# Four graph layers: tiles on 512-byte lines, and the third layer's wide product in blocks of 384, 384 and 260 columns

## The reference

```
h = maximum(layernorm(x), 0); x = x + L0(h, adj)   # attention, 8 heads, 6 static masks, 2 from adj
h = maximum(layernorm(x), 0); x = x + L1(h, adj)   # attention, 4 heads, masked by adj
h = maximum(layernorm(x), 0); x = x + L2(h, adj)   # graph attention, 4 heads:
    Wh = h @ W.T + bW;  e = Wh @ attn;  A = tanh(where(adj, e @ Wh.T, 0));  hp = relu(A @ Wh)
    ha = concat(hp) @ A_w.T;  hf = h @ fc_w.T
    coeff = sigmoid(hf @ g1_w.T + ha @ g2_w.T + gbias);  L2 = hf * coeff + ha * (1 - coeff)
h = maximum(layernorm(x), 0); x = x + L3(h, adj)   # attention times a cosine adjacency, 8 heads
```

## The kernel before, in words

| tile | start mod 512 | used as |
|---|---|---|
| ln_hT_hi, ln_hT_lo | 416 | moving and weights, all layers |
| square_w_hi, _lo | 416 | moving and weights, second and fourth layer |
| l0_w_hi, _lo | 480 | moving and weights, first layer |
| l0_oT, l1_oT | 256 | weights, output projections |
| l2_g_w_hi, _lo | 480 | weights |
| l2_wh_w_hi, l2_wh_w_lo | 480, 0 | moving; rows of 4112 bytes, so a second row lies 16 bytes further |
| l2_cat, l2_ha, l2_hf (hi, lo) | 416 | moving |
| l2_aw, l2_sq (hi, lo) | 32 | weights |
| same_batch | 192 | weights |

## Time and profile before

### The profile page before, as it was taken

One profiled execution on the slowest core, in us unless ns is written; L12 is line 12 of the kernel. 1 busy time (PEld: TensorE's weight loads), 2 busy tenths in 40 slices (PEclk: granted clock), 3 DMA queues, 4 the chain that ended last, 5 costly groups with the idle time before them and its releaser, 6 DMA issues. The chain is left out here.

```text
span 2171.3 us, 52286 instructions
## 1 busy us (share of the span) xinstructions
PE 2089.0 (96%) x18300; PEld 1881.0 (87%) x18300; DVE 1494.9 (69%) x3312; ACT 1002.0 (46%) x2057; POOL 504.2 (23%) x562
## 2 busy tenths in 40 slices
PE   7999999799999889999999999999999899999997
PEld 6888888699999789999999999999998778777786
DVE  6877878677777545555555555555554799999997
ACT  5666666454555322222222222222222476667665
POOL 3222222222222011111111110111111444444442
PEclk9999999999999899999999999999999999999999
DMA  3222222333222201111001001111110121122111
GB/s 90 80 71 63 74 68 65 118 113 84 81 82 86 68 21 31 31 30 30 30 30 30 25 20 30 30 30 30 30 30 20 42 61 51 53 59 59 55 49 45
DMA packets 149370, 113.31 MB, mean 52 GB/s; under 512 B 42944, under 2 KB 148800, under 8 KB 149312
## 3 DMA queue, kind: packets, MB, share of 16 engines
q1 hardware_dynamic: 149312, 112.52, 18.1%
HBM read 78.93 MB, written 33.55 MB: 52 GB/s over the span
## 5 line engine op out<-in xcount | busy, mean ns | idle before, releaser
L273 POOL TENSOR_TENSOR ln_rstd<-ln_var_eps,minus_half 128x2 f32<-128x2 f32 x128 | 90.9, 710 | 1106.2 <-DVE ln_var_eps L266 1106.2
L1615 ACT ACTIVATE l_cat_hi<-banks 128x512 fp32r<-128x512 f32 x128 | 76.5, 597 | 260.4 <-PE banks L1788 260.4
L161 PE MATMUL banks<-ln_hT_hi,square_w_hi 128*128 128x256 f32 x512 | 154.8, 302 | 5.0 <-DVE square_w_lo L614 3.2
L290 ACT ACTIVATE ln_h<-ln_x,ln_shift,ln_rstd 128x256 f32<-128x256 f32 x256 | 139.4, 592 | 32.0 <-DVE ln_shift L280 23.3
L161 PE MATMUL banks<-ln_hT_hi,l_g_w_hi 128*128 128x256 f32 x512 | 149.3, 292 | 4.9 <-POOL l_a_bd L1568 4.9
L163 PE MATMUL banks<-ln_hT_hi,square_w_lo 128*128 128x256 f32 x512 | 146.0, 285 | 0.0
L162 PE MATMUL banks<-ln_hT_lo,square_w_hi 128*128 128x256 f32 x512 | 145.7, 285 | 0.0
L161 PE MATMUL banks<-l_cat_hi,l_aw_hi 128*128 128x256 f32 x512 | 144.2, 282 | 1.4 <-DVE l_cat_lo L1675 1.4
L163 PE MATMUL banks<-l_cat_hi,l_aw_lo 128*128 128x256 f32 x512 | 144.1, 281 | 0.0
L162 PE MATMUL banks<-l_cat_lo,l_aw_hi 128*128 128x256 f32 x512 | 143.8, 281 | 0.0
L163 PE MATMUL banks<-ln_hT_hi,l_g_w_lo 128*128 128x256 f32 x512 | 143.1, 279 | 0.0
(11 more groups left out here) (227 smaller groups left out, 6910.8 us busy)
## 6 DMA issues: line engine op xcount, KB each, us to landing
hidden<-y SPq DMA_DIRECT2D x96, 256.0 KB, 2.2
ln_x<-hidden SPq DMA_DIRECT2D x96, 256.0 KB, 2.8
x_res<-hidden SPq DMA_DIRECT2D x96, 256.0 KB, 2.9
ln_x<-x SPq DMA_DIRECT2D x32, 256.0 KB, 2.9
x_res<-x SPq DMA_DIRECT2D x32, 256.0 KB, 3.0
out<-y SPq DMA_DIRECT2D x32, 256.0 KB, 2.2
l_adj_u<-adj SPq DMA_DIRECT2D x96, 16.0 KB, 2.4
l_stage_attnT<-L_attnT SPq DMA_DIRECT2D x4, 256.0 KB, 3.3
```

What stands on the lines that cost most here:

```text
L161: nc.tensor.matmul(out, lhs(lh), rhs(rh), start=start, stop=False, skip_group_check=True)
L273: self.nc.gpsimd.tensor_tensor(self.rstd[:, g.slot], self.var_eps[:, g.slot], self.core.minus_half[:, 0:PAIRS], ALU.pow).then_inc(self.rst ...
L290: last = self.nc.scalar.activation(self.h[:, u, p, :], self.x[:, u, p, :], ACT.Relu, bias=self.shift[:, u, p:p + 1], scale=self.rstd[:, u, ...
L1615: nc.scalar.activation(cat_hi[:, h * KC:(h + 1) * KC], halves(B_HP[h]), ACT.Relu).then_inc(cat_hi_ready.sem, 1)
```

## The change

Every SBUF tile is now asked for through `tile`, which places those with at least 128 elements a partition at a multiple of 512 bytes and smaller ones at 32. The rows of the third layer's wide weights (hi and lo) are lengthened from 1028 to 1152 columns and the rows of wh from 1028 to 1152, so that the second row begins on a multiple of 512 bytes as well; the added columns are neither written nor read. The wide product is cut at 384 and 768. The bias row keeps its 1028 columns. The same two-argument replacement stands at every place that makes a tile; the diff below leaves repeats out.

```diff
+LINE = 512
+
+
+def tile(nc, name, shape, dtype):
+
+    return nc.sbuf_tensor(name, shape, dtype, align_bytes=LINE if math.prod(shape[1:]) >= P else 32)
...
-        self.x_res = ctx.enter_context(nc.sbuf_tensor("x_res", [P, 2, PAIRS, D], F32))
-        self.y = ctx.enter_context(nc.sbuf_tensor("y", [P, 2, PAIRS, D], F32))
+        self.x_res = ctx.enter_context(tile(nc, "x_res", [P, 2, PAIRS, D], F32))
+        self.y = ctx.enter_context(tile(nc, "y", [P, 2, PAIRS, D], F32))
...
-        sb = lambda n, shape, dt=F32: ctx.enter_context(nc.sbuf_tensor(f"ln_{n}", shape, dt))
+        sb = lambda n, shape, dt=F32: ctx.enter_context(tile(nc, f"ln_{n}", shape, dt))
...
-        H, CH, WC = 4, 4 * KC, 4 * D + 4
+        H, CH, WC = 4, 4 * KC, 4 * D + P
...
-        self.wh_bias = sb("wh_bias", [P, WC])
+        self.wh_bias = sb("wh_bias", [P, 4 * D + 4])
...
-    THIRDS = ((0, 344), (344, 344), (688, WC - 688))
+    THIRDS = ((0, 384), (384, 384), (768, WC - 768))
...
-        wh = sb("wh", [P, PAIRS, WC])
+        wh = sb("wh", [P, PAIRS, H * D + P])
```

More of the change, by code:

```diff
@@ L1 @@
+import math
 from contextlib import ExitStack
@@ L320, in __init__ @@
     def __init__(self, core, ctx, tag, raw):
-        sb = lambda n, shape, dt=F32: ctx.enter_context(core.nc.sbuf_tensor(f"{tag}_{n}", shape, dt))
+        sb = lambda n, shape, dt=F32: ctx.enter_context(tile(core.nc, f"{tag}_{n}", shape, dt))
         self.raw = sb("w_raw", [P, raw, KC, D])
@@ L370, in attention_layer @@
     with ctx:
-        sb = lambda n, shape, dt=F32: ctx.enter_context(nc.sbuf_tensor(f"{tag}_{n}", shape, dt))
+        sb = lambda n, shape, dt=F32: ctx.enter_context(tile(nc, f"{tag}_{n}", shape, dt))
         w_stage, w_hi, w_lo = weights.raw, weights.hi, weights.lo
@@ L872, in place_constants @@
     ns = n - 3 * P
[L873 to L876, removed]
+    c = ctx.enter_context(tile(nc, "constants_sb", [P, n], F32))
+    core.ident_bf = ctx.enter_context(tile(nc, "ident_bf", [P, P], BF16))
+    core.static_mask = ctx.enter_context(tile(nc, "static_mask", [P, ns], BF16))
+    core.minus_half = ctx.enter_context(tile(nc, "minus_half", [P, 16], F32))
     core.ident = c[:, 0:P]
@@ L880, in place_constants @@
     same_batch = c[:, 2 * P:3 * P]
-    core.same_batch = ctx.enter_context(nc.sbuf_tensor("same_batch", [P, P], F32R))
+    core.same_batch = ctx.enter_context(tile(nc, "same_batch", [P, P], F32R))
     core.waits_passed = core.once("waits_passed")
@@ L906, in __init__ @@
         self.core, self.square, self.w, self.b = core, square, w, b
-        sb = lambda n, shape, dt=F32: ctx.enter_context(core.nc.sbuf_tensor(f"l3_{n}", shape, dt))
+        sb = lambda n, shape, dt=F32: ctx.enter_context(tile(core.nc, f"l3_{n}", shape, dt))
         self.block_w = sb("block_w", [P, P])
@@ L989, in gated_graph_layer @@
     with ctx:
-        sb = lambda n, shape, dt=F32: ctx.enter_context(nc.sbuf_tensor(f"l3_{n}", shape, dt))
+        sb = lambda n, shape, dt=F32: ctx.enter_context(tile(nc, f"l3_{n}", shape, dt))
         w_hi, w_lo = weights.square.hi, weights.square.lo
@@ L1448, in __init__ @@
         nc = core.nc
-        H, CH, WC = 4, 4 * KC, 4 * D + 4
-        sb = lambda n, shape, dt=F32: ctx.enter_context(nc.sbuf_tensor(f"l2_{n}", shape, dt))
+        H, CH, WC = 4, 4 * KC, 4 * D + P
+        sb = lambda n, shape, dt=F32: ctx.enter_context(tile(nc, f"l2_{n}", shape, dt))
         self.w = w
@@ L1456, in __init__ @@
         self.v_col = sb("v_col", [P, H, KC])
-        self.wh_bias = sb("wh_bias", [P, WC])
+        self.wh_bias = sb("wh_bias", [P, 4 * D + 4])
         self.half_gbias = sb("half_gbias", [P, KC])
         self.stage = ctx.enter_context(ExitStack())
-        sb = lambda n, shape, dt=F32: self.stage.enter_context(nc.sbuf_tensor(f"l2_stage_{n}", shape, dt))
+        sb = lambda n, shape, dt=F32: self.stage.enter_context(tile(nc, f"l2_stage_{n}", shape, dt))
         self.wb = sb("wb", [P, CH, D + 1])
@@ L1885, in graph_attention_setup @@
     with ExitStack() as ctx:
-        sb = lambda n, shape, dt=F32: ctx.enter_context(nc.sbuf_tensor(f"l2_stage_{n}", shape, dt))
+        sb = lambda n, shape, dt=F32: ctx.enter_context(tile(nc, f"l2_stage_{n}", shape, dt))
         wh_w = sb("wh_w", [P, KC, HD])
```

## The result

| | before | after |
|---|---|---|
| median, runs of both kernels on one chip | 2172.61 us (2171.58 to 2173.91, 4 runs) | 2188.6 us (2186.4 to 2190.11, 4 runs) |
| ratio, with its 95% interval | | 1.0067 (1.0054 to 1.008) |
| span of the profiled execution | 2171.3 us | 2188.2 us |

The change costs about 16 us. The forecast was 2125 us. What came is the rival "same place, slower", priced at 2192.

What follows compares the result with a forecast made beforehand. PE was taken to bound the first three layers, DVE the fourth. Savings of 41.0 (crossings), 1 (fourth layer) and 5.8 us (wide blocks), 47.8 together, gave a 2123.5 us span and a 2125 us forecast; range 2095 to 2192, its own 2108 to 2150.

Steps and rivals of the forecast that it cites:

- same place, slower: Rival for float32r products: weights and moving operand collide at small distance modulo 512; all go to 120 ns, +19 us, chance 0.27.
- What bounds the kernel: Claim that PE bounds the first three layers, busy 95% to 100%, and DVE the fourth, busy 94%, with PE slack.
- 3.2 ns a crossing and 1.8 in g: Assumed price, in float32r products, of each 512-byte line an operand crosses; two of three crossings go in 256-column products.
- the gain of 41 us in the sum: Fewer line crossings in the 256-column products of the first three layers, summed over 32 groups a layer: 41.0 us.
- the block of the earlier trace: The one wh_w_lo block of the wide product already on a line, running like its neighbour: 0.32 us for the two.
- four stretches of three layers agree on it: Reason for choosing 3.2 ns a crossing: four stretches of products lose 9.3 to 10.1 ns with three crossings each.
- What I held against it: Objection to the same-place rival: first-layer queries and keys, also at distance 64, show 118 ns in every other group.
- The rule of two independent read ports: Skill rule that loading weights takes no bandwidth from a running matmul; by it the same-place rival costs 0.
- Blocks of 384, 384 and 260: New cuts of the third layer's wide product: 6.2 ns of crossings in place of 11.2, saving 5.8 us.
- 109 ns: Assumed floor for a 256-column float32r product, from transposes at 110 ns each; 145 ns for the wide product.
- The full-floor rival: All float32r excess above 109 and 145 ns goes once both streams start on lines: 74 us, 2099 us, chance 0.17.
- Evacuation, DVE, plain float32, padding: Terms put at nothing; DVE evacuation 553 and 420 ns, DVE allowed 2 us and plain float32 4 us either way.

Runs made afterwards that it cites:

- e4: Changed kernel with product weights moved 64 bytes behind a 512-byte line and wh_w 192, all else on lines: 2155.72 us, ratio 0.991 to the kernel before.
- e5: e4 with the values and output matrices of the attention weights another 128 bytes further, so every distance is 64: 2150.24 us, ratio 0.9886 to the kernel before.
- e3: Changed kernel with all float32r operand tiles 64 bytes behind a 512-byte line, every distance still 0: 2187.41 us, ratio 1.0065 to the kernel before.
- e6: Changed kernel with only the weights of g moved to 64 bytes behind a line: 2178.66 us, ratio 1.002 to the kernel before.
- m1: Separate kernel without the layers: 256 series of 30 products, both operands placed in 32-byte steps; pitch 113.3 to 120.1 ns by distance modulo 256.
- m2: Separate kernel without the layers: 112 series, distance in 4-byte steps at 256 columns, then six other widths; 256 columns took 113.3 to 122 ns.
- m3: Separate kernel without the layers: series with 32 to 128 weights columns, then series behind different preceding products; at distance 64, 113.3 or 117.8 ns.
- e2: Changed kernel with the wide product's cuts back at 344 and 688: 2187.45 us, ratio 1.0061 to the kernel before.
- e1: Kernel before with only the wide product's cuts moved to 384 and 768, tiles unmoved: 2180.38 us against 2172.91, ratio 1.0027.

## Why the prediction was wrong, point by point

- *What bounds the kernel.* Right, though the stretch of 540 to 880 us, read as the second layer, takes in the preparation of the third layer's weights and over 100 us of the third. PE's pitches are the time in three layers. In the fourth they fell from 119.6 to 115.2 and 116.2 ns in e4 and e5, and the layer from its first to its last product of queries stayed at 449.0 and 449.4 us, against 449.6 before: DVE bounds it, PE's pitch is free there.
- *"3.2 ns a crossing and 1.8 in g."* This is the step that failed. There is no price of a crossing (e3, e6, m1), and the gain of 41 us in the sum hung on it. In its place the runs showed a price of the distance between weights and moving operand: 113.3 ns at 64 bytes, 117.8 to 120.1 at the others (m1). The change made every distance 0, so that g, forecast to fall to about 111 ns, rose from 114.1 to 119.7, ha from 118.6 to 119.5, and the whole by 16 us. The sign was in the working: g and the queries each needed a price of their own, 1.8 and 2.2, and both lie at distance 64; the block of the earlier trace rows had no gain from its line at all. That "four stretches of three layers agree on it" weighed nothing, since they had nearly the same number of crossings; their distances were 0, 32, 96, 128 and 192, whose pitches happen to lie within 2.2 ns (m1).
- *The rival "same place".* The quantity was right, the distance between the two operands, and so was the size, +19 us against +16. The period was wrong (256 bytes, not 512), and so was "where their distance is small": 96 and 160 bytes are as slow as 0 in m1, and 8 bytes are faster than 128 in m2. That two reads collide is not shown. By layer: first 4.6 us, measured 3.9; second 2.0, measured 0.9; the products of 256 columns in the third 12.3, measured 9.6 + 1.5 = 11.1. Each is a little too large, because the means after the change are 118.7 to 120.0 ns and not 120, and the second layer had 118.5 to 119.3 before and not 118.7 throughout.
- *What I held against it* was that queries and keys at distance 64 show 118 ns in every other group. m3 has the answer: 113.3 and 117.8 are the two modes of that distance. A spread at one distance was no evidence against distance; it needed a second cause beside it.
- *The rule of two independent read ports* (the Trainium skill, "TensorE: Matmul & The Clock Gate", section "Step-by-step: what each phase is for"), by which that rival would cost nothing, doesn't hold here as a statement on time: the address of the weights against that of the moving operand is worth 6.7 ns of 120 in m1. That the two meet at a port is still only argued; with a quarter of the weights most of the loss stayed (113.3 to 117.8 ns, against 117.8 to 120 with all of them and 106.7 for the columns).
- *Blocks of 384, 384 and 260.* Forecast -5.8 us; measured 36 x 1.3 ns x 32 = 1.5 us in the wide product, 0.9 us with the first and last product of each wide stretch counted in, and nothing in all (e2). What I had left out is that other blocks change the pace of the products behind them, ha above all (e1, +7 us on the old addresses). The evacuation, the weights' load and the waits were rightly put at nothing.
- *Floor.* "109 ns" was reached nowhere: no series with 256 columns came below 113.3, and the load alone takes 111.6. The full-floor rival rested on it. The rule of the Trainium skill (same page, section "Back-to-back issue gap"), 109.2 ns for 256 columns, is under every run here; the page itself gives it for a single matmul on its own, and says that in a stream the load of the weights counts too.
- *Evacuation, DVE, plain float32, padding.* Right, at 553 and 425 ns, with nothing to see elsewhere. No wait took anything.

**Still open**: why the distances rank as they do, and what the mode consists of; a stretch of 55 to 59 us between the last keys of the second layer and the first g, in which the third layer's weights are prepared, differs by up to 4 us between these kernels (1.7 us longer after than before). The granted clock from 715 to 775 us is 0.83 before, 0.80 after and 0.91 in e5, which has the shortest such stretch; whether the clock is the cause is not shown.

## What to carry to other kernels

Where TensorE is the bound and the sum of columns does not give its time, measure the pitch of each kind of product and set it beside the distance of its two operands (weights less moving, modulo 256 bytes), before touching an alignment. Aligning everything to one grid makes every distance 0, for 256 columns one of the three slowest of the eight in m1, though for 260, 384 and 512 columns the best or as good as the best (m2): the distance has to be measured for the width that the kernel uses. Weights 64 bytes behind the moving operand everywhere were worth 1.1% against the kernel before and 1.8% against the aligned one (0.9886 / 1.0067). When one theory needs a second price for the rows that don't fit, look first for a quantity that orders all rows with one.

## What the runs showed of the hardware that I had not expected

- The pitch of 256 float32r columns lies between 113.3 and 122 ns, and 4 bytes of distance can decide (m2: 113.3 at 52, 117.8 at 56).
- The same products at the same addresses run at 113.3 or 117.8 ns by what ran ahead of them, to the end of a series of 24 (m3).
- Steady pitches that don't wobble are 113.3, 116.7, 120.0, 156.7, 160, 173.3 and 226.7 ns: at 2.4 GHz 272, 280, 288, 376, 384, 416 and 544 cycles, all multiples of 8 and most of 16 (m1, m2).
- Products of 128 and of 192 columns cost the same 111.6 ns with 128 columns of weights, and 128 columns cost 60 with 64 or 32 (m2, m3).
